# Turning the last 64 gated columns on VectorE, with a new order of the last stage

## The chip, the cores and the metric

One core of one Trainium2 chip runs the whole program as one launch. The metric is the device time in microseconds, from the first to the last instruction with what lies around them. The kernel before took 301.75 us (median of 3 runs, 301.51 to 305.46). TensorE is called PE here, VectorE DVE, ScalarE ACT, GpSimd POOL and SyncE SP, as in the profile.

## The reference

448 tokens of 512 features go through three parts: a tokenizer (layer norm, 1024 to 512 product, layer norm), a quantised gated layer with residual, and a mixture of 32 experts with the best 8 of each token:

```
rw, sel = top_k(softmax(x @ router_w.T), 8);  rw = rw / sum(rw)
for e, wg, wu, wd in experts:
    w_e = sum(where(sel == e, rw, 0))
    h = silu(x @ wg) * (x @ wu)          # 192 columns
    acc = acc + (h @ wd) * w_e[:, None]
out = h_residual + acc
```

All of it is in fp32 but the quantised layer. The change lies in the expert part and in the last sum.

## The kernel before

The engines' programs are written out by hand, and semaphores alone order them. One expert is one tile `t` (0 to 31) of up to 128 tokens, found by a rank, fetched by a gather from DRAM (`gather`, POOL) and added back to one of two sums in DRAM by an indirect DMA that adds (`scatter`, POOL; even tiles to one sum, odd ones to the other). What an expert has over 128 tokens goes into a last pass with lists (`Quad`), which starts behind tile 31.

For a tile, PE turns the gathered rows in four products with the identity (`transpose_x`, line 1195), multiplies by gate and up weights (`gate_up`, L1174), ACT takes the silu (L882), DVE multiplies gate, up and the token's share (`weigh`, L1652) into `hid`, 128 tokens x 192. For the down product these 192 columns must lie on partitions: PE turns the first 128 (L1227) and, in a second product (L1230), the last 64, DVE copies both out of PSUM into `h_t` (`turn_back`, L1657, 256 columns), and PE multiplies (`down_two`: L1202 for the first 128, L1205 for the last 64 of two tiles). The second product turns a stretch of 128 columns so placed that the 64 wanted ones come out on partitions 0 to 63 for an even tile and 64 to 127 for an odd one; both tiles' last weights share one buffer that way.

PE works in pairs: at an even `t` it does `transpose_h(t-1)`, `down_two(t-2)` (tiles t-2 and t-1), `transpose_h(t)`. Beside that each tile looks up a later tile's tokens: PE spreads a row of ranks (`place_row`, L1158), DVE compares it with the token numbers (`find`, L1638, then the index L1641), and the index lets POOL gather and PE go on to the next `place_row`, which waits for it. DVE's program in a tile is: `turn_back(t-1)` if t is even, `weigh(t)`, `find`, `turn_back(t)` if t is even, `keep(t)` (L1647). At t = 4 DVE works out from counts which experts need lists (`list_owners`, L1670 to L1679) and at t = 8 where these lie (`list_sought`, L1695, L1697). PE has a wait on the first (`table_read`) and on the second (`table_ready`) between `down_two` and `transpose_h(t)` of those tiles.

In the end ACT reads both DRAM sums back as one transfer each (L917) when the last scatters have landed, then copies the lists' result (L892); PE spreads it over the tokens in eight products, two for each quarter of the tokens (L1243); DVE adds it to `h` (`grown`, L1751), adds the first sum (L1756), then the second (L1761); SP stores three quarters and ACT the last one (L446).

Of the kernel before, what the change touches and what calls it, by code (L numbers as in the profile page):

```python
# [9 lines left out]
ALU = mybir.AluOpType  # L10
# [13 lines left out]
P = 128  # L24
# [94 lines left out]
def program(nc, x, w_tok, vecs, gb1, w_in, w_down, g_down, w_router, ffn, out):  # L119
# [3 lines left out]
    with ctx:  # L123
# [211 lines left out]
        ld_part = [sem(f"ld_part{n}") for n in range(2)]  # L335
# [72 lines left out]
        with_h_ready = sem("with_h_ready")  # L408
# [8 lines left out]
        xt_ready = sem("xt_ready")  # L417
        silu_ready = sem("silu_ready")
# [7 lines left out]
        act_out_done = sem("act_out_done")  # L426
# [15 lines left out]

        def store(eng, g, n_pairs, done):

            eng.wait_ge(fin_ready, 4 * n_pairs + g)
            eng.dma_start(out_v[:, g, :], result[:, g, :]).then_inc(done, 16)  # L446


        @block.sync
        def _(sp):  # L450
# [58 lines left out]
            for g in range(NG):  # L509
                sp.wait_ge(row_ready, g + 1)  # L510
                sp.dma_start(rows_v[:, g, 0:D], rows[:, g, 0:D]).then_inc(rows_out, 16)
            sp.wait_ge(gate_ready, NG)
            sp.dma_start(rows_v[:, :, D:ROW], rows[:, :, D:ROW]).then_inc(rows_out, 16)
            sp.wait_ge(z_done, NG)
            sp.wait_ge(xt_done, 1)
            load_expert(10)
# [10 lines left out]
            for g in range(NG - 1):  # L527
                store(sp, g, n_pairs, out_done)
            sp.wait_ge(out_done, 16 * (NG - 1))
# [3 lines left out]
        def _(pool):  # L533
# [144 lines left out]
            for k, n_pairs in pairs_of(pool, pairs_i, table_ready):  # L678
                for i in range(2):
                    gather(Quad(k + 1, i))  # L680
            for i in range(2):
                pool.wait_ge(ld_got[i], 16 * n_pairs + 16 * (NE // 8 + 1))
# [3 lines left out]
        def _(act):  # L686
# [222 lines left out]
            for k, n_pairs in pairs_of(act, pairs_i, table_ready):  # L909
                two = [Quad(k, 0), Quad(k, 1)]  # L910
                for m in two:
                    act.wait_ge(gu_done, m.lists(3))
                    silu(m)
                act.wait_ge(fin_ready, 4 * k + 3)
                for m in two:
                    act.wait_ge(added[m.i], 16 * (NE // 2))
                    act.dma_start(part[m.i][:, :, :], acc_v[m.i]).then_inc(ld_part[m.i], 16)  # L917
                for m in two:
                    y_list_out(m)
                for i in range(2):  # L920
                    x_turned(Quad(k + 1, i))
            store(act, NG - 1, n_pairs, act_out_done)
            act.wait_ge(act_out_done, 16)


        @block.tensor
        def _(pe):
# [270 lines left out]
            def down_two(t):  # L1198
# [4 lines left out]
                for m in (Tile(t), Tile(t + 1)):  # L1203
                    rows_ = rest_rows(m.slot)
                    nc.tensor.matmul(bank(4 + m.two), h_t[rows_, m.two, 1, :], pair_rest_of(m.slot), start=False, stop=True  # L1205
# [30 lines left out]
            def spread_lists(two):  # L1236

                for g in range(NG):
                    for m in two:
                        if g == 0:  # L1240
                            pe.wait_ge(y_ready, m.upto(-1))
                            pe.wait_ge(where_ready, 2 * m.k + (m.i + 1))
                        last = nc.tensor.matmul(bank(g)[0:G, :], where[:, m.i, g * G:(g + 1) * G], y_list[:, m.i, :],  # L1243
                                                start=m.i == 0, stop=m.i == 1)
                    last.then_inc(spread_done, 1)
# [79 lines left out]
        def _(dve):  # L1325
# [376 lines left out]
            for t in range(NE):  # L1702
# [6 lines left out]
                weigh(m, got[:, got_at(m.eight), D + t:D + t + 1])  # L1709
                if sought_in(t):  # L1710
# [5 lines left out]
                if t == 8:  # L1716
# [3 lines left out]
                    nc.vector.tensor_copy(pairs_f[:, :], pairs_i[:, :]).then_inc(fin_ready, 3)  # L1720
# [9 lines left out]
            for k, n_pairs in pairs_of(dve, pairs_i, table_ready):  # L1730
# [22 lines left out]
                def with_first(g):  # L1753
                    dve.wait_ge(ld_part[0], 16 * k + 16)
                    dve.wait_ge(h_ready, 4 * k + (g + 5))
                    nc.vector.tensor_tensor(part[0][:, g, :], part[0][:, g, :], h[:, g, :], ALU.add).then_inc(with_h_ready, 1)  # L1756

                def finished(g):
                    dve.wait_ge(ld_part[1], 16 * k + 16)
                    dve.wait_ge(with_h_ready, 4 * k + (g + 1))  # L1760
                    nc.vector.tensor_tensor(result[:, g, :], part[0][:, g, :], part[1][:, g, :], ALU.add).then_inc(fin_ready, 1)  # L1761

                grown(0)
                with_first(0)
                grown(1)
                with_first(1)
                grown(2)
                with_first(2)
                finished(0)
                finished(1)  # L1770
                grown(3)
                with_first(3)
                finished(2)
                finished(3)

# [39 lines left out]
```

## Time and profile before

| | |
|---|---|
| median of 3 runs | 301.75 us |
| the profiled execution | 302.17 us |
| its span, first to last instruction | 300.4 us |
| PE busy | 278.0 us (93%) |
| DVE / ACT / POOL busy | 151.1 / 125.2 / 127.7 us |
| mean granted TensorE clock | 0.981 |

A timeline row gives the start, the duration, the engine, the line, the operation, what is written from what, the shape and the count; in brackets stands how long the engine was idle before it and what ended that. A row with a count merges neighbours on one engine. An fp32 product shows as two entries. `scrap`, `w_t`, `big`, `ring`, `raw` and `last` are large pieces of SBUF that hold other tensors one after another: in the expert part `w_t` holds `x_t`, `hid`, `h_t`, `y`, and `scrap` the gathered rows. `ps` is PSUM.

### The profile page before, as it was taken

How to read it: one execution, taken by the hardware profiler on the slowest of the kernel's cores; microseconds unless marked ns; L12 is line 12 of the kernel's file. 1: busy time of each engine (PE TensorE's matmuls, PEld its weight loads, DVE VectorE, ACT ScalarE, POOL GpSimd, SP SyncE). 2: the span in 40 equal slices, each digit the busy share in tenths (PEclk: the TensorE clock that was granted, in tenths of full speed). 3: DMA queues.
4: the chain of work that ended last, by engine and by line, in shares of the span. 5: the costliest groups of instructions: out<-in, count | busy, mean ns of one | idle time of the engine just before them, and what ended most of it. 6: DMA issues, size and time to landing. Idle time of an engine off the chain costs nothing.

```text
span 300.4 us, 3845 instructions
## 1 busy us (share of the span) xinstructions
PE 278.0 (93%) x1159; PEld 147.6 (49%) x1159; DVE 151.1 (50%) x446; ACT 125.2 (42%) x213; POOL 127.7 (43%) x130
## 2 busy tenths in 40 slices
PE   4899999869999988999999999999999999999792
PEld 1335444536557445546545655565555545553131
DVE  2657999997798705263343332333243223114345
ACT  2346999899984412213321332133213321331101
POOL 3162210976542133253546445654366436434400
PEclk9999999999999599999999999999999999999979
DMA  7999999501979087599999999999999999966773
GB/s 241 319 412 422 378 406 333 245 0 38 422 280 324 14 268 271 176 303 280 305 311 344 326 341 344 371 336 347 345 365 323 336 303 324 331 122 96 139 176 125
DMA packets 19478, 83.67 MB, mean 279 GB/s; under 512 B 3476, under 2 KB 3604, under 8 KB 13345
## 3 DMA queue, kind: packets, MB, share of 16 engines
q1 hardware_dynamic: 11440, 64.77, 57.5%
q0 software_dynamic: 7488, 16.58, 24.6%
q10 hardware_dynamic: 530, 2.08, 2.7%
q8 instruction: 10, 0.16, 0.2%
q14 instruction: 10, 0.08, 0.1%
HBM read 72.34 MB, written 12.92 MB: 284 GB/s over the span
## 4 chain that ended last, share of the span: by engine, by line
PE 35%; DMA 26%; DVE 18%; issue 5%; ACT 4%; POOL 1%; POOLq 0%; DVEq 0%; ACTq 0%
DMA sum<-w_t,add_idx 22%; PE ps L1174 16%; PE ps L1202 5%; PE ps L1195 3%; PE ps L1205 3%; DMA ring<-sum 3%; DVE big L1456 2%; DVE stats L1340 2%; PE ps L1061 2%; DVE raw L1462 2%; PE ps L1227 1%; DMA scrap<-token_rows,idx 1%; PE ps L1158 1%; DVE scrap L1421 1%; ACT last L814 1%
## 5 line engine op out<-in xcount | busy, mean ns | idle before, releaser
L661 POOL DMA_INDIRECT sum<-w_t,add_idx x32 | 51.3, 1602 | 55.6 <-ACT w_t L888 40.9
L877 ACT ACTIVATE w_t<-ps 128x512 f32<-128x512 f32 x36 | 21.3, 598 | 76.3 <-PE ps L1195 76.1
L648 POOL DMA_INDIRECT scrap<-token_rows,idx x28 | 29.5, 1053 | 28.6 <-DVE add_idx L1647 13.9
L1657 DVE COPY w_t<-ps 128x256 f32<-128x256 f32 x34 | 14.4, 424 | 53.6 <-PE ps L1230 52.4
L1652 DVE SCALAR_TENSOR_TENSOR w_t<-ps,scrap,w_t 128x192 f32<-128x192 f32 x32 | 13.2, 413 | 54.1 <-issue 44.9
L882 ACT ACTIVATE w_t<-ps 128x192 f32<-128x192 f32 x34 | 11.3, 331 | 54.2 <-PE ps L1174 48.8
L1174 PE MATMUL ps<-ring,w_t 128*128 128x384 f32 x96 | 33.1, 487 | 0.7 <-ACT w_t L877 0.7
L566 POOL TENSOR_TENSOR root_out<-root_in,minus_half 112x1 f32<-112x1 f32 x20 | 13.1, 654 | 46.6 <-DVE root_in L1357 46.6
L965 PE MATMUL ps<-raw,last 128*112 128x512 f32 x64 | 31.3, 643 | 0.0
L1174 PE MATMUL ps<-big,w_t 128*128 128x384 f32 x88 | 30.2, 486 | 0.0
L1195 PE MATMUL ps<-ident,scrap 128*128 128x128 f32 x144 | 23.0, 284 | 2.1 <-DVE h L1751 1.8
L1195 PEld LDWEIGHTS ps<-ident,scrap 128*128 128x128 f32 x144 | 21.1, 206 | 7.3 <-issue 6.0
L1174 PEld LDWEIGHTS ps<-ring,w_t 128*128 128x128 f32 x96 | 17.4, 192 | 10.4 <-ACT w_t L877 0.9
L1638 DVE SCALAR_TENSOR_TENSOR hit<-ps,iota_p,token 128x448 f16<-128x448 f32 x32 | 21.6, 676 | 1.4 <-PE ps L1263 1.0
L1023 PE MATMUL ps<-w_t,scrap 128*112 128x512 bf16 (+1 forms) x96 | 20.5, 363 | 1.7 <-DVE raw L1462 1.2
L888 ACT ACTIVATE w_t<-ps 128x512 f32<-128x512 f32 x31 | 17.4, 597 | 9.1 <-PE ps L1205 5.5
L965 PEld LDWEIGHTS ps<-raw,last 128*112 128x112 f32 x64 | 11.8, 192 | 18.4 <-issue 18.4
L1174 PEld LDWEIGHTS ps<-big,w_t 128*128 128x128 f32 x88 | 16.0, 191 | 8.7
L577 POOL TENSOR_TENSOR big<-raw,scrap 112x704 f32<-112x704 f32 (+1 forms) x7 | 12.7, 1825 | 8.7 <-DVE raw L1462 8.7
L1023 PEld LDWEIGHTS ps<-w_t,scrap 128*112 128x112 bf16 x96 | 11.9, 130 | 8.5 <-DVE raw L1462 1.4
L646 POOL DMA_INDIRECT scrap<-token_rows,idx x8 | 7.8, 979 | 17.5 <-DVE idx L1641 10.5
L723 ACT ACTIVATE scrap<-big 128x1536 bf16<-128x1536 f32 (+1 forms) x8 | 11.0, 1378 | 6.7 <-DMA big<-in_mlp_w_in 6.2
(216 smaller groups left out, 472.7 us busy)
## 6 DMA issues: line engine op xcount, KB each, us to landing
big<-in_ffn SPq DMA_DIRECT2D x12, 1024.0 KB, 9.3
ring<-in_ffn SPq DMA_DIRECT2D x9, 1280.0 KB, 7.5
ring<-in_ffn SPq DMA_DIRECT2D x4, 1024.0 KB, 9.9
raw<-in_ffn SPq DMA_DIRECT2D x4, 1024.0 KB, 9.0
last<-in_ffn SPq DMA_DIRECT2D x4, 1024.0 KB, 10.1
big<-in_ffn SPq DMA_DIRECT2D x3, 1280.0 KB, 8.0
big<-in_mlp_w_in SPq DMA_DIRECT2D x2, 1536.0 KB, 18.1
big<-in_mlp_w_in SPq DMA_DIRECT2D x2, 1280.0 KB, 20.7
```

Of the source, the lines that this page charges most:

```text
L648: nc.gpsimd.indirect_dma_start(got[:, got_at(s), :], None, rows_dram[:, :], rows_, bounds_check=TOK - 1, oob_is_err=False).then_inc(ld_got ...
L661: nc.gpsimd.indirect_dma_start(acc_dram[m.two][:, :], bass.IndirectOffsetOnAxis(ap=add_idx[:, m.eight:m.eight + 1], axis=0), y[:, m.four, ...
L877: nc.scalar.activation(x_t[:, m.two, :, :], bank(2 + m.two).rearrange("p (c t) -> p c t", c=4), ACT.Copy).then_inc(xt_ready, 1)
L888: nc.scalar.activation(y[:, m.four, :], bank(4 + m.two), ACT.Copy).then_inc(y_ready, 1)
L965: last = nc.tensor.matmul(acc, patch_t[g % 2][:, c, :], wtok_raw[:, c, :], start=False, stop=c == KC - 1)
L1023: last = nc.tensor.matmul(bank(3 * half_, 3)[0:G, a:a + w], q1_t[:, c, g * G:(g + 1) * G], w_t4[:, c, half_ * I1 + a:half_ * I1 + a + w], ...
L1174: last = nc.tensor.matmul(dst, x_t[:, m.two, c, :], wg[:, :, c, :], start=c == 0, stop=c == 3)
L1195: last = nc.tensor.transpose(bank(2 + m.two)[:, c * P:(c + 1) * P], got[:, got_at(m.eight), c:D:4], ident[:, :])
L1202: nc.tensor.matmul(bank(4 + m.two), h_t[:, m.two, 0, :], down_of(m.slot), start=True, stop=False)
L1638: nc.vector.scalar_tensor_tensor(hit[:, :], bank(b)[:, 0:TOK], mine, token[:, :], ALU.is_equal, ALU.mult, accum_out=idx_f[:, s:s + 1]).the ...
L1652: nc.vector.scalar_tensor_tensor(hid[:, m.two, 0:IE], bank(m.two)[:, IE:2 * IE], gate, sg[:, :], ALU.mult, ALU.mult).then_inc(hid_ready, 1)
L1657: nc.vector.tensor_copy(h_t[:, m.two, :, :], bank(6)[:, 0:2 * P].rearrange("p (c t) -> p c t", c=2)).then_inc(ht_ready, 1)
```

## The change

For a tile, PE's second product is gone, `turn_back` copies 128 columns instead of 256, and DVE gets `turn_rest(t)` between `weigh(t)` and `find`: eight 32 x 32 transposes, from the last 64 columns of `hid` straight into the place in `h_t`. It waits for `weigh` and, because that place is free only then, for the down product of tile t-2. PE's last products wait for `rest_ready`. The lists keep their products.

The last stage: SP reads the two sums back in four quarters each, POOL adds the two quarters as they come, DVE adds the lists' result to `h` for all quarters, leaves its loop and adds POOL's result in four more steps; SP does all four stores. ACT has no transfers left there, so its copies of the lists' result stand right behind its silu. PE's eight spreading products run in another order. SP issues the load of expert 10 ahead of the store of the routing weights (before, behind it and behind a wait on `xt_done`).

```diff
@@ SP
+            sp.wait_ge(z_done, NG)
+            load_expert(10)
             sp.wait_ge(gate_ready, NG)
             sp.dma_start(rows_v[:, :, D:ROW], rows[:, :, D:ROW]).then_inc(rows_out, 16)
-            sp.wait_ge(z_done, NG)
             sp.wait_ge(xt_done, 1)
-            load_expert(10)
             load_expert(11)
...
+            for n in range(2):
+                sp.wait_ge(added[n], 16 * (NE // 2))
+                for g in range(NG):
+                    sp.dma_start(part[n][:, g, :], acc_v[n][:, g, :]).then_inc(ld_part[n][g], 16)
+            for g in range(NG):
+                sp.wait_ge(fin_ready, g + 1)
+                sp.dma_start(out_v[:, g, :], result[:, g, :]).then_inc(out_done, 16)
@@ POOL
+            for g in range(NG):
+                for n in range(2):
+                    pool.wait_ge(ld_part[n][g], 16)
+                nc.gpsimd.tensor_tensor(part[0][:, g, :], part[0][:, g, :], part[1][:, g, :], ALU.add).then_inc(both_ready, 1)
@@ ACT
-                act.wait_ge(fin_ready, 4 * k + 3)
-                for m in two:
-                    act.wait_ge(added[m.i], 16 * (NE // 2))
-                    act.dma_start(part[m.i][:, :, :], acc_v[m.i]).then_inc(ld_part[m.i], 16)
@@ PE
                     rows_ = rest_rows(m.slot)
+                    pe.wait_ge(rest_ready, m.upto())
...
-                nc.tensor.transpose(bank(6)[:, 0:P], hid[:, m.two, 0:P], ident[:, :])
-                if isinstance(m, Tile):
-                    a = P - IB * m.two
-                    last = nc.tensor.transpose(bank(6)[:, P:2 * P], hid[:, m.two, a:a + P], ident[:, :])
-                else:
+                last = nc.tensor.transpose(bank(6)[:, 0:P], hid[:, m.two, 0:P], ident[:, :])
+                if isinstance(m, Quad):
...
+                for g, i in ((0, 0), (1, 0), (0, 1), (2, 0), (1, 1), (3, 0), (2, 1), (3, 1)):
@@ DVE
+            def turn_rest(m):
+                dve.wait_ge(hid_ready, m.upto())
+                wait(dve, y_done, m.upto(-2))
+                for a in range(0, P, 32):
+                    for b in range(0, IB, 32):
+                        last = nc.vector.transpose(h_t[m.two * IB + b:m.two * IB + b + 32, m.two, 1, a:a + 32],
+                                                   hid[a:a + 32, m.two, P + b:P + b + 32])
+                last.then_inc(rest_ready, 1)
...
+                if isinstance(m, Tile):
+                    nc.vector.tensor_copy(h_t[:, m.two, 0, :], bank(6)[:, 0:P]).then_inc(ht_ready, 1)
+                    return
...
                 weigh(m, got[:, got_at(m.eight), D + t:D + t + 1])
+                turn_rest(m)
                 if sought_in(t):
                     find(sought_in(t))
...
+                for g in range(NG):
+                    grown(g)
+            for g in range(NG):
+                dve.wait_ge(both_ready, g + 1)
+                dve.wait_ge(h_ready, 4 * n_pairs + (g + 1))
+                nc.vector.tensor_tensor(result[:, g, :], part[0][:, g, :], h[:, g, :], ALU.add).then_inc(fin_ready, 1)
```

DVE's instructions of tile 8, from `weigh` to the table that PE waits for, before:

```order
L1652 SCALAR_TENSOR_TENSOR w_t<-ps,scrap,w_t 128x192 [waits ht_done,silu_ready,ld_got0]
L1638 SCALAR_TENSOR_TENSOR hit,idx_f<-ps,iota_p,token 128x448 [waits place_done]
L1641 TENSOR_SCALAR idx<-idx_f,no_row 128x1 [waits hit_ready]
L1695 TENSOR_SCALAR sought<-ps,iota_p 32x24 [waits tables_done]
L1695 TENSOR_SCALAR sought<-ps,iota_p 32x24 x3
L1697 CAST owner_row<-ps 1x96
```

and now:

```order
L1648 SCALAR_TENSOR_TENSOR w_t<-ps,scrap,w_t 128x192 [waits ht_done,silu_ready,ld_got0]
L1656 STREAM_TRANSPOSE w_t<-w_t 32x32 [waits y_done,hid_ready]
L1656 STREAM_TRANSPOSE w_t<-w_t 32x32 x7
L1634 SCALAR_TENSOR_TENSOR hit,idx_f<-ps,iota_p,token 128x448 [waits place_done]
L1637 TENSOR_SCALAR idx<-idx_f,no_row 128x1 [waits hit_ready]
L1703 TENSOR_SCALAR sought<-ps,iota_p 32x24 [waits tables_done]
L1703 TENSOR_SCALAR sought<-ps,iota_p 32x24 x3
L1705 CAST owner_row<-ps 1x96
```

Eight transposes stand ahead of the look-up and the table, and the first of them waits for a down product. PE's instructions of the same tile, from the lists' table products to the next expert's rows, now:

```order
L1253 MATMUL ps<-shift,ones 128x96 [waits owner_ready,ht_ready]
L1254 MATMUL ps<-owner,iota_e 1x96
L1199 MATMUL ps<-ring,w_t 128x512 [waits y_ready,ht_ready]
L1199 MATMUL ps<-raw,w_t 128x512 [waits y_ready,ht_ready]
L1203 MATMUL ps<-ring,w_t 128x512 [waits rest_ready] x2
L1225 MATMUL ps<-ident,w_t 128x128 [waits ht_ready,hid_ready,table_ready]
L1192 MATMUL ps<-ident,scrap 128x128 [waits xt_ready,ld_got2]
```

The wait for the table stands right behind the products whose end lets DVE begin its transposes; the second turning product (L1230 before) is gone from between the last two rows.

## Rows read from the trace of the kernel before

**Rows 1.** Window of 130 to 265 us, PE: width, busy (entries), clock, DMA share, GB/s.

```profile
130.00:265.00 135.00, 134.34 (x518) 1.00 1.03 327
```

**Rows 2.** Chain that ended last: start, us, what.

```profile
207.14 9.11 DMA sum<-w_t,add_idx
...
281.83 8.06 DMA ring<-sum
```

**Rows 3.** Timeline of one settled pair of tiles, PE and DVE.

```profile
188.83 0.42 DVE L1652 SCALAR_TENSOR_TENSOR w_t<-ps,scrap,w_t 128x192 f32<-128x192 f32 x1 [3.00 <-issue]
189.17 0.68 DVE L1638 SCALAR_TENSOR_TENSOR hit<-ps,iota_p,token 128x448 f16<-128x448 f32 x1
...
191.45 0.27 PE L1227 MATMUL ps<-ident,w_t 128*128 128x128 f32 x1
...
191.56 0.27 PE L1230 MATMUL ps<-ident,w_t 128*128 128x128 f32 x1
...
191.87 0.42 DVE L1657 COPY w_t<-ps 128x256 f32<-128x256 f32 x1 [1.71 <-PE ps L1230]
```

**Rows 4.** Timeline of tiles 0 to 2, index on DVE and place_row on PE.

```profile
113.01 0.21 DVE L1641 TENSOR_SCALAR idx<-idx_f,no_row 128x1 int32<-128x1 f32 x1
...
113.28 0.36 PE L1158 MATMUL ps<-w_t,ident 128*128 128x448 f16 x1
...
118.02 0.36 PE L1158 MATMUL ps<-w_t,ident 128*128 128x448 f16 x1 [1.14 <-DVE idx L1641]
```

**Rows 5.** Timeline of tile 4, with list_owners on DVE.

```profile
131.07 0.42 DVE L1657 COPY w_t<-ps 128x256 f32<-128x256 f32 x1 [1.31 <-PE ps L1230]
...
131.55 0.22 PE L1250 MATMUL ps<-n_over,before_e 32*32 32x1 f32 x2 [0.33 <-DVE w_t L1657]
...
131.74 0.68 DVE L1638 SCALAR_TENSOR_TENSOR hit<-ps,iota_p,token 128x448 f16<-128x448 f32 x1
...
132.75 0.15 DVE L1671 COPY start<-ps 32x1 f32<-32x1 f32 x1
...
133.66 1.13 PE L1205 MATMUL ps<-big,w_t 64*128 64x512 f32 x4
```

**Rows 6.** Timeline of tile 8, with list_sought on DVE.

```profile
152.24 0.68 DVE L1638 SCALAR_TENSOR_TENSOR hit<-ps,iota_p,token 128x448 f16<-128x448 f32 x1
...
153.09 0.99 DVE L1695 TENSOR_SCALAR sought<-ps,iota_p 32x24 f32<-32x24 f32 x4
...
154.10 0.24 DVE L1697 CAST owner_row<-ps 1x96 int32<-1x96 f32 x1
...
154.24 1.13 PE L1205 MATMUL ps<-ring,w_t 64*128 64x512 f32 x4
154.38 0.35 DVE L1686 COPY pick<-owner 32x128 f16<-32x128 f16 x2
```

**Rows 7.** Timeline around tile 31's turn and down product.

```profile
268.20 0.33 PE L1227 MATMUL ps<-ident,w_t 128*128 128x128 f32 x1 [0.40 <-DVE w_t L1652]
...
268.68 0.42 DVE L1657 COPY w_t<-ps 128x256 f32<-128x256 f32 x1 [0.47 <-PE ps L1230]
...
269.33 1.02 PE L1202 MATMUL ps<-raw,w_t 128*128 128x512 f32 x2
```

**Rows 8.** Timeline of the last stage: spreading products, grown, last store.

```profile
284.77 8.81 PE L1243 MATMUL ps<-scrap,ranked 128*112 128x512 f32 x16 [1.91 <-ACT scrap L892]
...
294.46 0.68 DVE L1751 TENSOR_TENSOR h<-h,ps 112x512 f32<-112x512 f32 x1
...
297.10 0.33 ACTq L446 DMA_DIRECT2D out<-raw  x1
```

**Rows 9.** Window in the last stage: width, PE, PEld, DVE, ACT, POOL, clock, DMA share, GB/s.

```profile
285.00:289.00 4.00, 4.00 (x6) 1.45 (x6) 0.69 (x1) 0.13 (x1) 0.98 (x1) 0.59 0.99 248
```

**Rows 10.** Timeline of the routing weights' store on SP and the first gather on POOL.

```profile
100.32 0.72 SPq L513 DMA_DIRECT2D token_rows<-scrap  x1
...
103.51 1.21 POOL L646 DMA_INDIRECT scrap<-token_rows,idx  x1 [7.76 <-DVE idx L1641]
```

More of the change, by code:

```diff
@@ L334, in program @@
         added = [sem(f"added{n}") for n in range(2)]
-        ld_part = [sem(f"ld_part{n}") for n in range(2)]
+        ld_part = [[sem(f"ld_part{n}_{g}") for g in range(NG)] for n in range(2)]
         dve_chain = sem("dve_chain")
@@ L407, in program @@
         y_last = sem("y_last")
-        with_h_ready = sem("with_h_ready")
+        both_ready = sem("both_ready")
         h_ready = sem("h_ready")
@@ L417, in program @@
         xt_ready = sem("xt_ready")
+        rest_ready = sem("rest_ready")
         silu_ready = sem("silu_ready")
@@ L425, in program @@
         out_done = sem("out_done")
-        act_out_done = sem("act_out_done")
         block = ctx.enter_context(nc.Block())
@@ L441, in bcast @@
             return v.rearrange("(a n) -> a n", a=1).broadcast_to([G, n])
-        def store(eng, g, n_pairs, done):
-            eng.wait_ge(fin_ready, 4 * n_pairs + g)
-            eng.dma_start(out_v[:, g, :], result[:, g, :]).then_inc(done, 16)
         @block.sync
@@ L526, in _ @@
                     load_picked(bass.ds(e, 1), s)
-            for g in range(NG - 1):
-                store(sp, g, n_pairs, out_done)
-            sp.wait_ge(out_done, 16 * (NG - 1))
+            for n in range(2):
[5 more added lines that the diff above has]
+                sp.dma_start(out_v[:, g, :], result[:, g, :]).then_inc(out_done, 16)
+            sp.wait_ge(out_done, 16 * NG)
         @block.gpsimd
@@ L921, in _ @@
                     x_turned(Quad(k + 1, i))
-            store(act, NG - 1, n_pairs, act_out_done)
-            act.wait_ge(act_out_done, 16)
         @block.tensor
@@ L1236, in spread_lists @@
             def spread_lists(two):
[L1238 to L1245, printed above, removed]
+                for g, i in ((0, 0), (1, 0), (0, 1), (2, 0), (1, 1), (3, 0), (2, 1), (3, 1)):
+                    m = two[i]
+                    if g == 0:
+                        pe.wait_ge(y_ready, m.upto(-1))
+                        pe.wait_ge(where_ready, 2 * m.k + (m.i + 1))
+                    last = nc.tensor.matmul(bank(g)[0:G, :], where[:, m.i, g * G:(g + 1) * G], y_list[:, m.i, :],
+                                            start=m.i == 0, stop=m.i == 1)
+                    if m.i == 1:
+                        last.then_inc(spread_done, 1)
             def list_starts():
@@ L1719, in _ @@
                         pick_lists(Quad(0, i))
-                    nc.vector.tensor_copy(pairs_f[:, :], pairs_i[:, :]).then_inc(fin_ready, 3)
                     dve.sem_inc(h_ready, 4)
@@ L1751, in grown @@
                     nc.vector.tensor_tensor(h[:, g, :], h[:, g, :], bank(g)[0:G, :], ALU.add).then_inc(h_ready, 1)
[L1753 to L1774, printed above, removed]
+                for g in range(NG):
[4 more added lines that the diff above has]
+                nc.vector.tensor_tensor(result[:, g, :], part[0][:, g, :], h[:, g, :], ALU.add).then_inc(fin_ready, 1)
 def laid_out(x, w_tok, b_tok, g1, b1, g2, b2, w_in, g_in, w_down, g_down, w_router, we_gate, we_up, we_down):
```

## The prediction, on record before the changed kernel ran

> **What bounds the kernel now.** I read the engines' table, then windows, the chain of waits, and timelines. In the expert loop PE is busy 134.34 of 135 us at full clock, and the DMA engines are full as well, with a share of 1.03 [rows 1]. The chain that ended last runs through the adding scatters: they show as pieces of 9.11 us one behind the other, and then as the 8.06 us in which the sums are read back [rows 2]. Two things thus end almost together, PE's products and the scatters; PE waits almost nowhere, so whatever is added to its waits moves its end by as much. DVE is busy half of the time, so its *sum* of work is no bound. The question is where PE waits for it, and that is read from the places where an index or a table goes from DVE to PE.
>
> **What is taken away.** The second turning product starts 0.11 behind the first and holds PE for as much [rows 3]. There are 32; the one of tile 0 lies ahead of a wait that covers it, so 31 x 0.11 = **-3.4 us**. The copy in `turn_back` shrinks from 256 to 128 columns. With 0.42 for 256 columns and 0.15 for one [rows 3, 5] I take 0.29 for it, 0.13 less. It counts only where a copy is late.
>
> **The price of a transpose.** No row shows one. Four instructions of DVE on 24 columns that move from one group of 32 partitions to the next take 0.99, so 0.25 each, with no overlap; two copies that stay on one group take 0.35, which is 0.17 each [rows 6]. Other neighbours on DVE overlap by 0.08 [rows 3], which makes 0.13 of an instruction of 0.21 [rows 4]. An estimate by length: 0.15 for one column [rows 5] and 32 columns at 1.05 ns (0.42 less 0.15 over 255), once or twice, gives 0.18 to 0.22. The eight transposes of a tile write two groups of partitions in turn and read four, so the four instructions without overlap are the nearest row, and I take a step of **0.21**, 1.7 us for a tile. Ends: 0.13 (1.0 us) and 0.25 (2.0 us).
>
> The Trainium skill, "VectorE: DVE Perf Modes", in the section on two Vector instructions with no wait between them, says that an instruction that starts on another quadrant than the last input or output starts only when all before it have finished. That speaks against this way of writing the loop; by it the step is the whole duration and the time is my forecast's, without it that of the first rival. The four instructions of rows 6 agree.
>
> **Where the 1.7 us meet PE.** In a settled pair they are hidden. In an odd tile DVE ends its work 1.71 before `turn_back` can start [rows 3]; 1.7 plus 0.13 for the wait on `weigh` and the lost overlap just fills it, and the shorter copy gives 0.13 back. In an even tile the first transpose waits for the down product of tile t-2, which delays `find` by some 2.8, but PE needs that index only behind the next `gate_up`, and what queues behind on DVE (`find`, `turn_back`, `keep`) is done in time. If that cover were short, each 0.1 would cost 0.1 a tile. At the start and at the tables there is no cover:
> - Tile 0: `place_row` starts at 113.28 with its index done at 113.22 [rows 4]. The index comes 1.8 later (1.7 and 0.13): **+1.8**.
> - Tile 1: PE waits already 1.14 for the index of `find` [rows 4], which stands behind `turn_rest`: **+1.8** more.
> - Tile 3: `turn_back` has 1.31 of slack [rows 5], and PE waits for it: 1.8 - 1.31 - 0.13 = **+0.4**.
> - Tile 4: the first transpose waits for the down product of tile 2, done half-way through the last four entries, at about 134.3 [rows 5]. Then 1.7, then from `find` to the end of the copy of `start` 132.90 - 131.74 = 1.16: the table is there at 137.2, and PE wants it at 133.66 + 1.13 = 134.79 [rows 5]: **+2.4**. Before it came at 132.90 and cost nothing.
> - Tile 8: likewise 154.8 (half-way through the row at 154.24) + 1.7 + (154.34 - 152.24 = 2.10) = 158.6 against 154.24 + 1.13 = 155.37 [rows 6]: **+3.3**.
> - Tile 31: `turn_rest` and `keep` stand ahead of the last `turn_back`: from the end of `weigh`, which PE awaited until 268.20, over 1.7, 0.15 for `keep` and 0.29 to 270.34, against a product that began at 269.33 [rows 7]; of this 0.4 goes off, since PE's wait of 0.40 there came from ACT behind a scatter's landing, and with PE late that scatter is in time. I put **+0.5**.
>
> The loop's sum: -3.4 + 1.8 + 1.8 + 0.4 + 2.4 + 3.3 + 0.5 = **+6.8**.
>
> **The clock.** The four new waits of PE last 1.8, 2.9 (with the 1.14 of before), 2.4 and 3.3. Behind the one idle stretch of such a length, 1.91 [rows 8], the granted clock fell to the lower level, 1.2 GHz, and was 0.59 on the mean over 4 us of full work [rows 9]; that is (1 - 0.59) x 4 = 1.6 lost. The idle 1.14 [rows 4] was followed by none. I take two falls of the possible four: **+3.3**. Ends: none, and three (4.9).
>
> **The start.** The first gather starts 1.0 behind the landing of the store of the weights issued at 100.32 [rows 10]. The load of expert 10 now goes into the same queue ahead of that store: 512 x 384 and 192 x 512 in fp32 are 1.18 MB, 3.6 us at the 327 GB/s of rows 1. It is issued behind `z_done`, a few us earlier than the store, and so is nearly through by then: **+0.3**, between 0 and 1. That it comes earlier is worth nothing, since PE waits for no load.
>
> **The end.** ACT now copies the lists' result without its transfers ahead, so the eight products start at 284.77 - 1.91 = 282.86 [rows 8], at full clock: 8.81 - 1.6 = 7.2 gives 290.1. `grown` of the last quarter to 290.8, some 0.4 for leaving the loop, four adds of 0.65: the last store at 293.8 against 297.10 [rows 8]: **-3.3**. The other way to this store is the sums: the last quarter lands as late as the second sum did, which I put near 292 (2 behind the 289.89 at which the first one's 8.06 end [rows 2]), and POOL's four adds (if each takes twice DVE's 0.68) follow from 288 on and end at 294. So at equal lateness the two ways are level, and with PE late by seven to ten the spreading products decide; the scatters, which are not late by as much, have slack then.
>
> **Sum** against the profiled execution (302.17, span 300.4): 302.17 + 6.8 + 3.3 + 0.3 - 3.3 = 309.3. That execution was 0.42 above the median, so **308.8 us** against 301.75.
>
> **Rivals.**
> - *Transposes that overlap*, a step of 0.13. The waits become 1.1, 1.1, 0, 1.7, 2.7 and 0, the loop +3.2; with one clock fall 1.6, the start and the end: +1.8, **303.5 us**. For it speaks every other pair of neighbours on DVE, against it the four instructions of rows 6. The Trainium skill, same page, in its table of cycles, gives 58 cycles and one for each column, at 0.96 GHz: an estimate of 0.09 for a block, by which the time would be near 302; the page itself calls that too low, and the 0.15 for one column in rows 5 is above it. Chance 0.20.
> - *Waits as forecast, no clock fall*: 308.8 - 3.3 = **305.5 us**. For it: PE does something in between each time. Chance 0.13.
> - *Long transposes*, a step of 0.25: waits 2.1, 2.1, 0.7, 2.8, 3.7 and 0.8, the loop +8.8, three clock falls 4.9: **312.2 us**. Chance 0.15.
> - *The other side: DVE's turns are ready before PE asks, everywhere.* Then -3.4 and -3.3 stand alone: 301.75 - 6.7 = **295.0 us**, faster by 2.2%. It decides at tile 8: PE waits unless table and transposes end within 155.37 - 154.8 = 0.57 of the down product, and the look-up alone takes 2.10. It would need PE to be held elsewhere, by scatters, for as long. Chance 0.04.
> - The forecast: chance 0.48.
>
> **How the numbers follow.** The forecast with the time of its own case, 308.8; its own range is 306.5 to 311. The overall range goes from just below the overlapping case to past the long one, **302 to 314**, and leaves out the faster side and a fourth clock fall. A measurement of this kernel tells 2%, 6 us, from no change: slower is above 307.8, faster below 295.7. Slower: the long case and two thirds of the forecast, 0.15 + 0.33 = 0.48. Within 2%: the rest of the forecast and the two rivals between, 0.15 + 0.20 + 0.13 = 0.48. Faster: 0.04.
>
> **What would show it.** In the profile after: transposes on DVE whose starts are as far apart as they last (0.2), not nearer; a wait of PE of 1.8 ahead of the second tile's `place_row` and near 3 ahead of the third's; waits of 2.4 and 3.3 ahead of the turning product of tiles 4 and 8, ended by DVE; a pair of tiles 0.22 (2 x 0.11) shorter later on; a granted clock below 1 behind one or two of these waits; spreading products that follow the lists' products at once, at full clock. I am wrong if PE's pair gets longer (then DVE or the scatters set it), if PE passes the tables without a wait, or if the last stage is bound by POOL's adds.

## The result and the profile after

The changed kernel takes 325.17 us (median of 4 runs, 323.17 to 325.76) beside 303.61 for the kernel before on the same chip: a ratio of 1.0795, 95% interval 1.0753 to 1.0838. It is slower, by three times what was forecast. Some executions of a kernel are a few per cent slower than its others; medians here are of all executions, ratios and their intervals of the fast ones alone, so that a ratio need not be the quotient of the medians. The profiled execution took 325.76 us, its span 323.9; the span before was 300.4, so 23.5 us are to be found.

Windows of the kernel after. Columns: window, width, busy time of PE, PEld, DVE, ACT and POOL with entries, granted clock, DMA share, GB/s:

```profile
130.00:180.00 50.00, 41.35 (x136) 22.43 (x135) 26.97 (x124) 10.49 (x23) 16.95 (x13) 0.86 0.76 250
130.00:265.00 135.00, 122.91 (x433) 65.61 (x431) 77.75 (x348) 33.82 (x71) 60.65 (x46) 0.95 0.91 290
```

Where PE was busy 134.34 of 135 us [rows 1] it is busy 122.91, at a mean clock of 0.95, and the DMA engines are no longer full. The waits of PE after (what waited, for what, us in total, times, longest) say on whom:

```profile
PE ps L1155 <- DVE idx L1637: 9.0, 13, 3.0
PE ps L1225 <- DVE owner_row L1705: 4.0, 1, 4.0
PE ps L1225 <- DVE start L1679: 3.1, 1, 3.1
```

All three end with DVE: 13 waits of `place_row` for an index, and one for each table. The timeline of tile 8 after answers to [rows 6]:

```profile
164.86 1.13 PE L1203 MATMUL ps<-ring,w_t 64*128 64x512 f32 x4
166.09 1.70 DVE L1656 STREAM_TRANSPOSE w_t<-w_t 32x32 f32<-32x32 f32 x8 [3.19 <-PE ps L1203]
167.83 0.68 DVE L1634 SCALAR_TENSOR_TENSOR hit<-ps,iota_p,token 128x448 f16<-128x448 f32 x1
168.69 0.99 DVE L1703 TENSOR_SCALAR sought<-ps,iota_p 32x24 f32<-32x24 f32 x4
169.69 0.24 DVE L1705 CAST owner_row<-ps 1x96 int32<-1x96 f32 x1
169.99 0.48 PE L1225 MATMUL ps<-ident,w_t 128*128 128x128 f32 x1 [4.00 <-DVE owner_row L1705]
171.12 4.95 PE L1171 MATMUL ps<-big,w_t 128*128 128x384 f32 x8
```

DVE stood idle for 3.19 us with the look-up and the table behind its first transpose, then worked through them while PE waited. Behind that wait the eight products of `gate_up` take 4.95 in place of 2.75: half clock.

A settled pair after, its odd tile, answers to [rows 3]:

```profile
187.11 1.73 DVE L1656 STREAM_TRANSPOSE w_t<-w_t 32x32 f32<-32x32 f32 x8
188.87 0.69 DVE L1634 SCALAR_TENSOR_TENSOR hit<-ps,iota_p,token 128x448 f16<-128x448 f32 x1
189.28 0.27 PE L1225 MATMUL ps<-ident,w_t 128*128 128x128 f32 x1
189.60 0.22 DVE L1637 TENSOR_SCALAR idx<-idx_f,no_row 128x1 int32<-128x1 f32 x1
189.87 0.36 PE L1155 MATMUL ps<-w_t,ident 128*128 128x448 f16 x1 [0.32 <-DVE idx L1637]
```

`place_row` starts 0.59 behind `transpose_h`; before it was 0.22 (191.45 and the product at 191.67). So this place costs 0.37, the missing second product of the even tile gives 0.11 back, and the pair is 10.13 in place of 9.86 (distance of every second `weigh`, in both timelines).

From the starts of `weigh` in the two timelines (before / after: tile 0 at 111.95 / 112.54, tile 4 at 131.41 / 135.89, tile 5 at 138.69 / 149.04, tile 8 at 151.92 / 162.50, tile 9 at 159.26 / 176.52, tile 24 at 231.64 / 251.32, tile 31 at 267.73 / 291.74) the 23.5 us fall into stretches:

| stretch | forecast | measured |
|---|---|---|
| up to tile 0 | +0.3 | +0.6 |
| tiles 0 to 4, three late indices or copies | +3.6 | +3.9 |
| tile 4 to 5: wait for `start`, clock | +3.9 | +5.9 |
| tiles 5 to 8 | -0.3 | +0.2 |
| tile 8 to 9: wait for the table, clock | +4.8 | +6.7 |
| tiles 9 to 24, settled pairs | -1.7 | +2.4 |
| tiles 24 to 31 | -0.8 | +4.3 |
| tile 31 to the end, with tile 31's late copy | -2.8 | -0.5 |

(Both falls of the clock of the forecast are put to tiles 4 and 8 here.) The last stretch has two parts: the last scatter lands 17.4 us behind tile 31's `weigh`, before 15.9, and from there to the end of the span it takes 14.8 us, before 16.7. The end of the loop, in the chain after that ended last:

```profile
246.63 9.43 DMA sum<-w_t,add_idx
...
256.95 9.63 DMA sum<-w_t,add_idx
...
269.41 7.12 DMA sum<-w_t,add_idx
...
277.26 4.73 issue
281.99 0.43 DVE w_t L1648
...
303.02 6.08 DMA sum<-w_t,add_idx
309.12 3.37 DMA ring<-sum
```

and PE and ACT there:

```profile
281.08 0.60 ACT L891 ACTIVATE w_t<-ps 128x512 f32<-128x512 f32 x1 [2.45 <-DMA sum<-w_t,add_idx]
282.46 0.33 PE L1225 MATMUL ps<-ident,w_t 128*128 128x128 f32 x1 [1.14 <-DVE w_t L1648]
284.61 1.94 PE L1199 MATMUL ps<-ring,w_t 128*128 128x512 f32 x2 [0.95 <-DVE w_t L1663]
```

ACT's copy of `y` waits for a scatter's landing with the next silu behind it; so `weigh` is late, PE waits 1.14 and 0.95, and then works at half clock (two entries of the down product in 1.94, where rows 7 have 1.02).

The last stage after answers to [rows 8]:

```profile
307.70 7.12 PE L1238 MATMUL ps<-scrap,ranked 128*112 128x512 f32 x16
312.64 5.39 POOL L683 TENSOR_TENSOR ring<-ring 112x512 f32<-112x512 f32 x4 [1.75 <-DMA ring<-sum]
314.86 0.69 DVE L1759 TENSOR_TENSOR h<-h,ps 112x512 f32<-112x512 f32 x1 [0.17 <-PE ps L1238]
315.47 4.32 DVE L1766 TENSOR_TENSOR raw<-ring,h 112x512 f32<-112x512 f32 x4
316.94 3.19 SPq L527 DMA_DIRECT2D out<-raw  x4
```

The spreading products do run at full clock, 7.12 in place of 8.81, and 2.26 us of that are lost behind them: before, the span ended 6.8 behind their end, now 9.1. DVE has all of `h` at 315.55, and its last four adds take 4.32. The instructions one by one (shortest, median, longest in ns; first and last start):

```profile
L683 POOL TENSOR_TENSOR ring<-ring x4: 1267/1272/1712, 312.6 to 316.3; 112x512 f32<-112x512 f32 x4
L1766 DVE TENSOR_TENSOR raw<-ring,h x4: 676/1062/1749, 315.5 to 319.1; 112x512 f32<-112x512 f32 x4
```

None of DVE's four waits for POOL, whose adds are done at 313.91, 315.13, 316.36 and 318.03: DVE's first starts when its last add into `h` ends, each later one when DVE's own before it ends. The first two, which lie beside an add of POOL, take 1.45 and 1.75 us, the two behind POOL's last take 0.68 each. POOL's last, which lies beside DVE's second, takes 1.71 in place of 1.27. So two adds with all inputs in SBUF, one on each engine, make each other longer here; by what, no run here takes apart.

### The profile page after: what moved, and what is told of

It reads as the page before. It is cut to its first block, busy times and chain, and to the rows that moved or that the text cites. A ratio compares the mean times of both kernels' runs of the same rounds, so it can differ in the third digit from the quotient of the medians.

```text
span 323.9 us, 4063 instructions
## 1 busy us (share of the span) xinstructions
PE 282.5 (87%) x1127; PEld 146.0 (45%) x1127; DVE 198.5 (61%) x697; ACT 125.9 (39%) x213; POOL 133.1 (41%) x134
## 4 chain that ended last, share of the span: by engine, by line
DVE 28%; DMA 24%; PE 19%; issue 12%; ACT 4%; POOL 3%; DVEq 0%; POOLq 0%; ACTq 0%
DMA sum<-w_t,add_idx 21%; DVE w_t L1656 7%; PE ps L1171 6%; PE ps L1199 4%; PE ps L1203 3%; DVE hit L1634 2%; DVE big L1452 2%; DVE stats L1336 2%; PE ps L1058 2%; DVE raw L1458 2%; DVE w_t L1648 1%; PE ps L1192 1%; DMA scrap<-token_rows,idx 1%; POOL sum L660 1%; DMA ring<-sum 1%
## 5 line engine op out<-in xcount | busy, mean ns | idle before, releaser
L1656 DVE STREAM_TRANSPOSE w_t<-w_t 32x32 f32<-32x32 f32 x256 | 51.9, 203 | 45.2 <-PE ps L1203 41.6
L1171 PE MATMUL ps<-ring,w_t 128*128 128x384 f32 x96 | 35.4, 515 | 0.7 <-ACT w_t L880 0.7
L1648 DVE SCALAR_TENSOR_TENSOR w_t<-ps,scrap,w_t 128x192 f32<-128x192 f32 x32 | 13.2, 413 | 35.4 <-issue 25.5
L1171 PE MATMUL ps<-big,w_t 128*128 128x384 f32 x88 | 32.4, 514 | 0.0
L1192 PE MATMUL ps<-ident,scrap 128*128 128x128 f32 x144 | 23.8, 292 | 2.5 <-DMA scrap<-token_rows,idx 1.6
L1171 PEld LDWEIGHTS ps<-ring,w_t 128*128 128x128 f32 x96 | 18.6, 204 | 11.4 <-issue 1.8
L1171 PEld LDWEIGHTS ps<-big,w_t 128*128 128x128 f32 x88 | 17.1, 205 | 9.8 <-issue 1.8
L1225 PE MATMUL ps<-ident,w_t 128*128 128x128 f32 x34 | 10.7, 314 | 8.8 <-DVE owner_row L1705 4.0
L1155 PE MATMUL ps<-w_t,ident 128*128 128x448 f16 x28 | 10.0, 358 | 9.0 <-DVE idx L1637 9.0
L645 POOL DMA_INDIRECT scrap<-token_rows,idx x8 | 7.8, 979 | 22.4 <-DVE idx L1637 13.2
```

Of the source, the lines that this page charges most:

```text
L1171: last = nc.tensor.matmul(dst, x_t[:, m.two, c, :], wg[:, :, c, :], start=c == 0, stop=c == 3)
L1192: last = nc.tensor.transpose(bank(2 + m.two)[:, c * P:(c + 1) * P], got[:, got_at(m.eight), c:D:4], ident[:, :])
L1648: nc.vector.scalar_tensor_tensor(hid[:, m.two, 0:IE], bank(m.two)[:, IE:2 * IE], gate, sg[:, :], ALU.mult, ALU.mult).then_inc(hid_ready, 1)
L1656: last = nc.vector.transpose(h_t[m.two * IB + b:m.two * IB + b + 32, m.two, 1, a:a + 32], hid[a:a + 32, m.two, P + b:P + b + 32])
```

## The experiments

Theory A: the transposes stand ahead of the look-up on DVE, and each place where PE then waits costs its wait and, at the long ones, the clock. Rivals: the new last stage costs (B); scatters and loads would have held the loop anyway (C); 55 us more of DVE work cost wherever they stand (D). Ratios are to the kernel before, run beside each on the same chip.

**Old end, transposes in place.** The kernel before with `turn_rest`, `turn_back` and `transpose_h` of the change.

> The transposes on VectorE at their place in the change, with the last stage and the loads' order of the kernel before. If the loss comes from the transposes' place in DVE's queue (theory A), all waits of PE return: 3 and 4 us ahead of the turning products of tiles 4 and 8, each with some 5 us at half clock behind it, and the time is that of the changed kernel plus what the new last stage saved, 1 to 3 us: 326 to 328 us. If the new last stage or the earlier load of expert 10 costs (theory B), this kernel is well below 325, near 310.

325.94 us (four executions, 319.26 to 329.75), ratio 1.066 (1.047 to 1.084). The waits are all there: from tile 4 to 5 it takes 13.2 us and from 8 to 9 14.1, as in the changed kernel (13.2 and 14.0; before 7.3 and 7.3). The transposes alone bring 6.6% of the 8.0%, and the two intervals overlap; B falls as the main cause. In the profiled execution (329.75) the clock also fell behind the wait at tile 1, which it did not in that of the changed kernel; the last section has the rows.

**New end alone.** The changed kernel with both products on PE and no transposes.

> The new last stage and the earlier load of expert 10 alone, both turning products on PE as before. Theory A: the loop is the old one, the last stage 1 to 3 us shorter, 299 to 301 us. Theory B: slower than 303.6, up to 315.

303.97 us, ratio 1.0074 (1.0024 to 1.0125). Not a gain but a small loss: this expectation of A failed. Its last stage, in an execution of 308.28:

```profile
287.32 7.12 PE L1239 MATMUL ps<-scrap,ranked 128*112 128x512 f32 x16
...
294.35 5.83 POOL L682 TENSOR_TENSOR ring<-ring 112x512 f32<-112x512 f32 x4 [3.84 <-DMA ring<-sum]
...
295.75 5.58 DVE L1754 TENSOR_TENSOR raw<-ring,h 112x512 f32<-112x512 f32 x4 [0.58 <-POOL ring L682]
```

The products end at 294.44; POOL begins at 294.35, when the second sum's first quarter is there, and its adds start 1.22 to 1.67 apart. DVE waits for the first of them alone (the 0.58 above). Its own first three adds, beside POOL's, take 1.64, 1.75 and 1.74, the fourth, behind POOL's last, 0.68:

```profile
L682 POOL TENSOR_TENSOR ring<-ring x4: 1266/1490/1712, 294.3 to 298.5; 112x512 f32<-112x512 f32 x4
L1754 DVE TENSOR_TENSOR raw<-ring,h x4: 678/1694/1746, 295.7 to 300.7; 112x512 f32<-112x512 f32 x4
```

From the last scatter's landing to the end of the span it takes 17.7 us here, 16.7 before. The changed kernel's 14.8 is shorter than both: there the two sums' last scatters land 4.7 apart (304.38 and 309.10), here 2.4 (285.96 and 288.39), so that most of the first sum's reads are under way before the second's begin. That this is why is not shown.

**Tables first.** In tiles 4 and 8 `turn_rest` stands behind `list_owners` or `list_sought`.

```diff
-                turn_rest(m)
+                if t not in (4, 8):
+                    turn_rest(m)
...
+                if t in (4, 8):
+                    turn_rest(m)
                 if t % 2 == 0:
                     turn_back(m)
```

> The changed kernel, but in tiles 4 and 8 the transposes stand behind the look-up and the tables on DVE. Theory A: PE's waits of 3.06 and 4.00 us there and the half clock behind them go, which were 5.9 and 6.7 us between neighbouring tiles: 325 - 12.5 = 312 to 313 us. Rival (theory C: the adding scatters and the loads would have held the loop anyway, since the DMA engines are full): part of this comes back as waits for landings, and the time stays above 317.

315.65 us, ratio 1.047 (1.034 to 1.060); the span 313.3, 10.6 less than the changed kernel's. Tile 4 to 5 takes 7.15 and 8 to 9 7.27: both stalls are gone, 12.8 us. Of the 2.2 between 12.8 and 10.6, 0.65 lie ahead of tile 0 and 1.4 behind tile 31, where the stage behind the last landing takes 16.7 in place of 14.8. From tile 9 to 31 it takes 115.3, in the changed kernel 115.2: some pairs are long in both (10.56 at tile 13 and 11.50 at tile 23 here), but the stalls did not come back in the loop. A is right on the place. The waits for landings that C has come back aren't seen in this run, whose time stayed below C's 317.

**Transposes behind.** In an odd tile right behind the look-up, in an even one last of all.

```diff
-                turn_rest(m)
                 if sought_in(t):
                     find(sought_in(t))
+                if t % 2:
+                    turn_rest(m)
...
                 keep(m)
+                if t % 2 == 0:
+                    turn_rest(m)
```

> The changed kernel with every tile's transposes behind the look-up: in an odd tile right behind it, in an even tile last of all. Theory A: no index and no table is late any more; only turn_back of the odd tile is late by 0.1 to 0.2 a pair, which the missing product gives back: a pair of 9.8, and with the new last stage 299 to 301 us. Rival (theory D: 55 us more of work on DVE costs wherever it stands): a pair stays at 10.1 and the time at 306 or more.

306.06 us, ratio 1.013 (1.004 to 1.023). A settled pair:

```profile
170.19 0.21 DVE L1637 TENSOR_SCALAR idx<-idx_f,no_row 128x1 int32<-128x1 f32 x1
170.44 1.73 DVE L1656 STREAM_TRANSPOSE w_t<-w_t 32x32 f32<-32x32 f32 x8
171.76 0.27 PE L1225 MATMUL ps<-ident,w_t 128*128 128x128 f32 x1
171.87 0.35 PE L1155 MATMUL ps<-w_t,ident 128*128 128x448 f16 x1
172.27 0.28 DVE L1663 COPY w_t<-ps 128x128 f32<-128x128 f32 x1
```

The same eight transposes, in the same 1.73, and `place_row` waits for nothing: the pair is 9.64, which is 9.86 less two products. D falls. But at tiles 17, 19, 21, 23 and 25 it is 10.40, 9.89, 10.22, 10.17 and 10.44, and by tile 31 the loop is 3.7 us behind that of the kernel before, with 0.6 of them there at tile 0. Behind tile 31 this execution (308.98, the longest of the four) loses another 3.1: 2.3 until the last scatter lands and 0.8 in the new last stage.

**Even tiles in place.** Odd tiles behind the look-up, even ones as in the change, with the tables first.

> The changed kernel with the transposes of odd tiles behind the look-up and those of even tiles left between weigh and find (behind the tables in tiles 4 and 8). If the settled pair of 10.13 comes from the odd tile alone, whose look-up PE needs 1.6 us behind weigh, the pair is 9.64 here, although the even tile's transposes still wait some 2.7 us for the down product with find behind them; tile 0 (even) still costs its 1.8. The end as in the kernel with the tables first, less 0.5 a pair until the scatters bind: 308 to 311 us. If the even tile's wait matters, the pair stays above 9.9 and the time near 315.

307.93 us (two executions, 304.22 and 311.63, too few for a ratio; 305.06 before beside it). In the profiled one, 311.63, the pair is 9.64 from tile 5 to 12, but for the table's at tile 8, then the scatters' irregular 9.4 to 11.7. So an even tile's wait for the down product, some 2.7 us with DVE idle, costs nothing in a settled pair, and the 10.13 are the odd tile's alone. From tile 0 to 1 it takes 6.60 as in the changed kernel, 4.74 where tile 0 too stands behind.

**One copy in place of the eight transposes** (the last 64 columns aren't turned):

```diff
-                for a in range(0, P, 32):
-                    for b in range(0, IB, 32):
-                        last = nc.vector.transpose(...)
+                own = slice(m.two * IB, m.two * IB + IB)
+                last = nc.vector.tensor_copy(h_t[own, m.two, 1, :], hid[own, m.two, 0:P])
```

> The changed kernel with one copy of 64 x 128 in place of the eight transposes of a tile (the last 64 columns are not turned, the copied block stands where they should). Waits and order stay, only the work on DVE shrinks from 1.73 to about 0.3 us. If the work's length is what is late in the settled pairs and at the start, the pair is 9.64 and tiles 1 and 2 lose 0.4 each in place of 1.85 and 1.75; the wait for the down product stays, and PE still waits at tiles 4 and 8, for 1.6 and 2.6 us. 325 - 2.9 - 2.9 - a fall of the clock (3) or two - some 4 in the settled pairs: 310 to 313 us. If the wait for the down product were the whole cause, it would stay above 318.

309.66 us, ratio 1.019 (1.009 to 1.028). The waits for the tables are 1.5 and 2.4 in place of 3.06 and 4.00, and the pair is 9.64. So the wait for the down product alone makes about half of PE's wait at a table. Of the whole cost it makes less at tile 4, 1.3 of 5.9 us, where the clock stays up behind the wait (1.00 from 136 to 140 us), and 3.7 of 6.7 at tile 8, where it falls (0.50 from 159.5 to 162). In the settled pair it is the work alone.

**PE kept busy.** Behind the down products of tiles 4 and 8, ahead of the wait:

```diff
+                    if t in (4, 8):
+                        pe.wait_ge(xt_ready, t + 2)
+                        for _ in range({4: 14, 8: 19}[t]):
+                            nc.tensor.matmul(bank(3)[:, 0:TOK], ident16[:, 0:1].broadcast_to([128, 128]), place[:, :], ...)
```

> The changed kernel with 14 more products of place's kind (448 columns, 0.19 us apart) on PE behind the down products of tile 4 and 19 behind those of tile 8, into a bank that nothing reads; they fill most of the waits of 3.06 and 4.00 us and change nothing else. If the half clock behind these waits comes from PE's idleness, the eight products of gate_up behind each take 2.75 us again, not 5.13 and 4.95, and the steps between tiles 4 and 5 and tiles 8 and 9 shrink by 2.5 to 3 each: 325 - 5.5 = 319 to 320 us. If the clock falls for another cause (or what it costs is given back by the scatters), the time stays at 325.

321.03 us (2 runs), ratio 1.056 (1.046 to 1.066); the span is 5.0 less. PE at tile 4:

```profile
139.89 2.82 PE L1295 MATMUL ps<-w_t,ident 128*128 128x448 f16 x14
143.03 0.33 PE L1225 MATMUL ps<-ident,w_t 128*128 128x128 f32 x1 [0.31 <-DVE start L1684]
143.19 0.66 PE L1192 MATMUL ps<-ident,scrap 128*128 128x128 f32 x4
143.69 2.75 PE L1171 MATMUL ps<-ring,w_t 128*128 128x384 f32 x8
```

The table is as late as it was, and the eight products behind it take 2.75. From tile 4 to 5 it takes 10.31 in place of 13.15, from 8 to 9 11.36 in place of 14.02: the clock costs 2.8 and 2.7, the waits themselves 3.1 and 4.0.

**Another order of the eight.** In the change the destination's group of 32 partitions changes at each of the seven steps and the source's at three; here the destination's at one and the source's at seven.

```diff
-                for a in range(0, P, 32):
-                    for b in range(0, IB, 32):
+                for b in range(0, IB, 32):
+                    for a in range(0, P, 32):
```

> The changed kernel with the eight transposes of a tile in another order: four with the same destination group of 32 partitions, then the other four (the sources change each time). If a step of 0.21 comes from the change of the destination's group, it falls to 0.13 for six of the seven steps, eight take 1.2 in place of 1.73 us. If each transpose runs by itself in any order, it stays 1.73 and the time 325.

327.01 us (one run). The group of all transposes:

```profile
L1656 DVE STREAM_TRANSPOSE w_t<-w_t 32x32 f32<-32x32 f32 x256 | 51.9, 203 | 43.7 <-PE ps L1203 40.1
```

203 ns each as in the changed kernel, and starts 0.21 to 0.22 apart in both orders: changing the destination's group less often doesn't shorten the step. Since each of the eight blocks differs from every other in one of the two groups, no order keeps both, and what a step with neither changed would take isn't shown.

**Half loads.** The kernel with the transposes behind; the loads of experts 12 to 31 bring half of their columns.

```diff
+                cols = cols if t < R else cols // 2
                 sp.dma_start(slots[n][:, 0:cols], ffn[t, :, 0:cols]).then_inc(ld_gu[n], 16)
```

> The kernel with the transposes behind the look-up, in which the loads of experts 12 to 31 bring only the first half of their columns (the rest keeps an older expert's weights). In a pair some 1.2 of 3.3 MB are gone. If the DMA engines' bytes are what stretches the pair from 9.64 to 10.2 and more from tile 16 on, the scatters land in 5 to 7 us in place of 9.3, the pair stays 9.64 to the end of the loop, and the time falls from 306 by 3 to 6 us, to 300 to 303. If each sum's chain of one scatter after the other binds by itself, whatever the load, the latency stays near 9 and the time at 306.

300.89 us, ratio 0.997 (0.991 to 1.002). The window of 180 to 230 us with whole loads:

```profile
180.00:230.00 50.00, 49.39 (x182) 26.80 (x181) 30.84 (x139) 14.17 (x30) 25.61 (x21) 1.00 1.04 342
```

and with half:

```profile
180.00:230.00 50.00, 50.00 (x188) 27.86 (x187) 32.80 (x148) 14.49 (x31) 26.79 (x21) 1.00 0.92 232
```

The pair stays 9.64 to tile 26. From tile 14 to 18 the scatters of even tiles land in 5.0 to 5.6 us (with whole loads in 9.2 to 9.5). Those of odd tiles don't gain: at least 8.8 and 8.0 us for tiles 15 and 17 (8.5 and 8.6), and from tile 20 on even ones take 9.0 to 10.4 again. C is right in this much: with fewer bytes to load, nothing holds the loop above PE's 9.64 up to there. Why the two sums' scatters differ isn't shown.

**Transposes behind, old end.**

> The kernel before with the transposes in place of PE's second turning product, behind the look-up in odd tiles and last in even ones; last stage and loads' order as before. Theory C (scatters and loads bind as well): the pair is 9.64 until the adding scatters hold PE near tile 16, then 10.2 to 10.4, and the loop ends no earlier than that of the kernel before: 302 to 305 us beside 303 to 305. Rival: PE alone binds the loop: 31 x 0.11 = 3.4 us faster.

304.88 us, ratio 1.004 (0.999 to 1.009). In the best of places the transposes gain nothing that the runs can tell. 3.4 us of PE's time are off; from tile 0 to 22 the loop is 1.6 us ahead of that of the kernel before, from 22 to 31 it loses 2.6. The DMA engines are at 1.04 from 180 to 230 us, as before, with 348 and 349 GB/s.

**Quarters, added on DVE.** The kernel before; SP reads the sums back in quarters, ACT no longer does, DVE adds as before.

```diff
+                sp.wait_ge(fin_ready, 4 * k + 3)
+                for n in range(2):
+                    sp.wait_ge(added[n], 16 * (NE // 2))
+                    for g in range(NG):
+                        sp.dma_start(part[n][:, g, :], acc_v[n][:, g, :]).then_inc(ld_part[n][g], 16)
...
-                act.wait_ge(fin_ready, 4 * k + 3)
-                for m in two:
-                    act.wait_ge(added[m.i], 16 * (NE // 2))
-                    act.dma_start(part[m.i][:, :, :], acc_v[m.i]).then_inc(ld_part[m.i], 16)
```

> The kernel before with one thing changed in the last stage: SP instead of ACT reads the two sums back, in four quarters each, and all adds stay on DVE in the order of before. The lists' result is then copied at once, and the spreading products follow the lists' products by 0.1 in place of 1.9 us, at full clock. If what made the new last stage slow is POOL's adds (5.4 to 5.8 us for four, which begin only when the second sum's first quarter lands), this one ends 3 to 4 us before the kernel before. If the sums' landing bounds it anyway, at most 1 us.

300.54 us, ratio 0.995 (0.989 to 1.000). Its last stage:

```profile
284.18 7.12 PE L1244 MATMUL ps<-scrap,ranked 128*112 128x512 f32 x16
...
292.15 0.68 DVE L1752 TENSOR_TENSOR h<-h,ps 112x512 f32<-112x512 f32 x1
...
294.80 0.37 ACTq L446 DMA_DIRECT2D out<-raw  x1
```

From the last scatter's landing (285.52) to the end of the span it takes 13.0 us, against 16.7 before and 17.7 with POOL's adds. So the stage itself gains 3.7, within the 3 to 4 expected. The profiled execution as a whole gains 1.8, since its last scatter landed 1.9 later than in that of the kernel before (0.9 of it by tile 31), for which I have no cause. The interval of the ratio just reaches 1, so a gain of the whole is not quite shown.

**Both**: transposes behind, and this last stage.

> The transposes behind the look-up together with the last stage read in quarters by SP and added on DVE. By the runs so far the transposes there gain nothing (the scatters bind) and the last stage gains 1.5 to 3.5: 300 to 302 us, the same as that last stage on the kernel before (300.5) within 0.5%. If DVE's work were a burden by itself, 303 or more.

301.78 us beside 305.06: ratio 0.991 (0.986 to 0.997), faster than the kernel before by some 0.9%, well under the 2% that the prediction counts as a change. Its interval overlaps that of the last stage alone, so whether the transposes add to it isn't settled.

## Why the prediction was wrong

The direction was right, the place and the kind of the waits too; the size was 7 us against 21.6 by the medians of one chip, and the range ended at 314.

- **The price of a transpose**: 0.21 forecast, 0.214 from start to start and 203 ns each measured. Right, and with it the forecast of 1.7 for a tile (1.73).
- **Tiles 0, 1 and 3**: +1.8, +1.8 and +0.4 forecast, +1.9, +1.7 and +0.4 measured.
- **"In a settled pair they are hidden"** is the step that failed in kind. I took the slack of DVE up to `turn_back`, 1.71, and left out that PE needs the odd tile's *index* first: it was done at 190.10 and wanted at 191.67, a slack of 1.57 for 1.73 of transposes and the 0.16 around them, and 0.11 less still as the second product was gone. So the forecast's -0.22 a pair became +0.27. Over 15 tiles that and one longer wait of PE for the index (0.85 in place of 0.32, with `weigh` late behind a scatter's landing) make 4.1 of the difference. With the odd tile's transposes behind the look-up the pair was the forecast's 9.64.
- **The tables**: the waits are 3.1 and 4.0, not 2.4 and 3.3. I let the transposes start half-way through the last four entries; they started 0.10 behind their end (164.86 + 1.13 = 165.99 and 166.09), so 0.7 later in both places, and that is the difference.
- **The clock** was the right mechanism with too small a price. Two falls at 1.6 were forecast; there were three, 2.8 and 2.7 at the tables and some 1.8 near the end (1.94 + 1.96 for six entries that take 1.02 + 1.13). The price of 1.6 came from the one fall of before, whose eight spreading products lost 8.81 - 7.12 = 1.7; behind the longer waits here the clock stayed low longer, at tile 4 for all that PE did from 142.32 to about 148.2. The two forecast falls and the third make 4.0 of the difference.
- **"The scatters, which are not late by as much, have slack then"**: wrong. Tiles 24 to 31 were +4.3 against -0.8, 1.8 of it the third fall of the clock. A scatter of an even tile is a piece of 9.3 to 9.6 us, and the next on its sum is issued 0.9 behind its landing, so that sum goes on in steps of 10.2 to 10.5 us from the scatter of tile 12 to that of tile 22, a little more than PE's pair of 10.13; they started as late as PE did and could make up nothing. Rows 2 show these pieces before, rows 1 the full DMA engines; with half loads the even tiles' became short and the pair stayed PE's 9.64. This fits with -3.4 us of PE products bringing nothing.
- **The end**: -3.3 forecast for the stage, -0.5 measured behind tile 31 (-2.8 with the 0.5 of its late copy). The products did end 2.8 sooner behind tile 31's `weigh`, 23.1 against 25.9. The term that failed is "four adds of 0.65": DVE's four took 4.32 and not 2.6, because the first two lay beside POOL's. POOL's own add was put well at 1.36 (5.39 for four, 1.35 on the mean), but the forecast priced each engine by itself. With the new end alone, where PE was in time, the wait for the second sum's first quarter comes on top, which I had named as what would show me wrong.

No rival held the result. The one of long transposes had the nearest time, 312.2 (its own terms, 8.8 + 4.9 + 0.3 - 3.3 on 301.75, add up to 312.4), for a reason that is false.

## What to carry to other kernels

When work is put into an engine's queue, list everything that stands behind it on that queue and, for each, who wants it *first*; the nearest consumer in the code is not always the one with the least slack. With the old end, the same eight instructions cost 6.6% ahead of the look-up and nothing that the runs can tell behind it. Where PE and the DMA engines are both full, time taken from PE alone came back as waits, but waits added to PE weren't made up. Leave the last adds to the engine that needs 0.69 and not 1.27 us or more, and don't price two engines' adds one by one if they run side by side: here that made 0.68 into as much as 1.75.

## What was not expected of the hardware

A long wait alone doesn't tell whether TensorE's clock falls. Ahead of tile 2's `gate_up` in the changed kernel PE waited 3.02 us, after a wait of 1.89 that ended at 115.73, and the products behind it ran at 2.4 GHz:

```profile
122.35 0.36 PE L1155 MATMUL ps<-w_t,ident 128*128 128x448 f16 x1 [3.02 <-DVE idx L1637]
122.55 1.78 PE L1171 MATMUL ps<-big,w_t 128*128 128x384 f32 x5
```

In tile 4 it waited 3.06 us, and the eight behind ran at 1.2 GHz for 5.13 us, and near the end two waits of 1.14 and 0.95 had the same effect. Even the same wait, behind the same instructions, can go either way. The wait of 1.89 at tile 1 led to no fall in the changed kernel, and its eight products behind it took 2.74; with the old end the clock was 0.50 from 116 to 118 us:

```profile
115.12 0.38 PE L1159 MATMUL ps<-w_t,ident 128*128 128x448 f16 x1 [1.89 <-DVE idx L1640]
115.32 4.43 PE L1175 MATMUL ps<-big,w_t 128*128 128x384 f32 x8
```

What sets these apart no run here shows, so a forecast can give a fall only a chance, as this one did. The Trainium skill, "VectorE: DVE Perf Modes", in the section on two Vector instructions with no wait between them, has an instruction held until all before it have finished when an input of it starts in another quadrant (group of 32 partitions) than the last input from that memory did, or its output in another than the last output did. By that each transpose here is held in both orders, and the traces agree with it, 0.21 from start to start for 203 ns each. The table of cycles of the Trainium skill, "VectorE: DVE Perf Modes", in the section on the TRN2 errata, would make such an instruction 0.09 us, an estimate that the 203 ns contradict.
